# A transformer layer pipeline on one core: four written-out engine orders and the PSUM banks laid out anew, and the first input turned inside the first attention

## The reference, cut to what matters

```python
for i in range(DEPTH):                                        # 6
    x = attn_layer(shift_tokens(x), Wqkv[i], q_scale[i], k_scale[i], Wo[i]) + x
    x = ffn_layer(shift_tokens(x), ln_g[i], ln_b[i], W1[i], b1[i], W2[i], b2[i]) + x

def attn_layer(x, Wqkv, qs, ksc, Wo):                         # 16 heads of 64
    q, k, v = jnp.split(x @ Wqkv, 3, -1)
    q = l2norm(q) * qs
    k = l2norm(k) * ksc
    q = q * cos * scale + rotate_half(q) * sin * scale
    k = k * cos * inv + rotate_half(k) * sin * inv
    out = local_attention(q, k, v)                            # windows of 32, each sees itself and the one before
    return out @ Wo

def ffn_layer(x, g, bln, W1, b1, W2, b2):
    xn = (x - mu) / jnp.sqrt(var + 1e-05) * g + bln
    a, gate = jnp.split(xn @ W1 + b1, 2, -1)
    return a * gelu(gate) @ W2 + b2
```

## Time and profile before

| what | value |
|---|---|
| median of 3 runs | 1480.26 us (1478.79 to 1480.74) |
| the profiled execution, its own time | 1482.22 us |
| span of its instructions | 1480.4 us |
| PE matmul busy | 1422.5 us, 96%, 25844 instructions (214 of them before 54.4 us) |
| ACT busy | 1371.5 us, 93% |
| DVE busy | 1331.4 us, 90% |
| POOL busy | 1257.3 us, 85% |
| mean granted TensorE clock | 0.990 of full speed |

### The profile page before, as it was taken

How to read it: one execution, slowest core, us unless ns; L and a number is a source line. 1 busy time by engine, 2 the same in 40 slices (tenths; PEclk the granted TensorE clock), 3 DMA queues, 4 the chain that set the end, 5 groups by cost and what they waited for, 6 DMA issues and landing times.

```text
span 1480.4 us, 65611 instructions
## 1 busy us (share of the span) xinstructions
PE 1422.5 (96%) x25844; PEld 1278.0 (86%) x25844; DVE 1331.4 (90%) x2411; ACT 1371.5 (93%) x2797; POOL 1257.3 (85%) x1219
## 2 busy tenths in 40 slices
PE   6789999999999999999999999999999999999996
PEld 5578888988998899888888889888898899898886
DVE  7699899999999999999999999999999999999973
ACT  4488899999999999999999999999999999999995
POOL 5498889889898888989888888989898988888871
PEclk9799999999999999999999999999999999999999
DMA  5111121212122211212121221212122111111111
GB/s 150 38 49 52 49 59 49 59 41 62 43 64 58 65 45 49 65 49 64 52 57 44 57 70 51 60 52 54 43 57 68 45 50 41 48 35 51 51 35 40
DMA packets 96187, 80.30 MB, mean 54 GB/s; under 512 B 66282, under 2 KB 79598, under 8 KB 95854
## 3 DMA queue, kind: packets, MB, share of 16 engines
q1 hardware_dynamic: 94990, 75.34, 18.9%
q10 hardware_dynamic: 864, 0.26, 0.1%
HBM read 17.91 MB, written 1.05 MB: 13 GB/s over the span
## 4 chain that ended last, share of the span: by engine, by line
PE 57%; ACT 20%; issue 13%; DVE 9%; DMA 1%; ACTq 0%; POOL 0%; SPq 0%; DVEq 0%; POOLq 0%
PE bank L1132 45%; PE bank L1248 7%; ACT pz L727 4%; PE bank L1276 3%; DVE parts L951 3%; ACT bank L712 3%; ACT sq L651 2%; ACT es L719 2%; DVE n L961 2%; ACT ot L734 1%; DVE newton L970 1%; ACT qt L675 1%; ACT kt L675 1%; ACT gt L756 1%; ACT v L662 1%
## 5 line engine op out<-in xcount | busy, mean ns | idle before, releaser
L480 POOL TENSOR_TENSOR rot<-parts 128x512 f32<-128x512 f32 x384 | 492.0, 1284 | 79.7 <-DVE parts L951 75.9
L951 DVE TENSOR_TENSOR parts<-bank,rtab 128x1024 f32<-128x1024 f32 x384 | 464.7, 1211 | 0.3 <-issue 0.2
L491 POOL TENSOR_TENSOR rot<-rot,rnorm 128x512 f32<-128x512 f32 x384 | 398.6, 1044 | 54.1 <-DVE rnorm L977 54.1
L651 ACT ACTIVATE sq<-bank 128x512 f32<-128x512 f32 x384 | 233.0, 607 | 39.7 <-DVE n L961 20.0
L1132 PE MATMUL bank<-w_hi,x_hi 128*128 128x512 f32 x576 | 256.8, 446 | 7.7 <-DVE x_lo L943 6.7
L961 DVE TENSOR_REDUCE n<-sq 128x8 f32<-128x512 f32 x384 | 254.2, 675 | 4.2 <-ACT sq L651 4.0
L497 POOL TENSOR_TENSOR es<-es,r 128x512 f32<-128x512 f32 x192 | 200.5, 1044 | 37.5 <-DVE r L1003 31.7
L1132 PE MATMUL bank<-w_lo,x_hi 128*128 128x512 f32 x576 | 229.6, 399 | 0.0
L727 ACT ACTIVATE pz<-bank 64x512 f32<-64x512 f32 x384 | 226.2, 589 | 3.1 <-PE bank L1276 0.8
L1132 PE MATMUL bank<-w_hi,x_lo 128*128 128x512 f32 x576 | 228.9, 397 | 0.0
L1248 PE MATMUL bank<-ident,rot 128*128 128x128 f32 x1536 | 215.7, 274 | 5.1 <-issue 4.0
(11 more groups left out here) (91 smaller groups left out, 2985.7 us busy)
## 6 DMA issues: line engine op xcount, KB each, us to landing
vb<-v SPq DMA_DIRECT2D x96, 384.0 KB, 3.7
w_new<-in_Wqkv SPq DMA_DIRECT2D x36, 256.0 KB, 3.0
vb<-v SPq DMA_DIRECT2D x48, 128.0 KB
w_o<-in_Wo SPq DMA_DIRECT2D x12, 256.0 KB
xin<-x_tok SPq DMA_DIRECT2D x48, 64.0 KB, 2.1
xs<-x_tok SPq DMA_DIRECT2D x48, 64.0 KB, 2.7
xin<-x_tok SPq DMA_DIRECT2D x48, 56.0 KB, 2.1
xs<-x_tok SPq DMA_DIRECT2D x48, 56.0 KB, 2.1
```

The lines of the kernel that those rows point to most:

```text
L480: g.tensor_tensor(rot[:, i * CH:(i + 1) * CH].rearrange(halves, z=2, c=HD), parts[:, b:b + CH].rearrange(halves, z=2, c=HD), parts[:, b + ...
L491: g.tensor_tensor(c, c, over(r, CHH, DH), ALU.mult).then_inc(s_sc[i], 1)
L651: a.activation(sq[:, (i % 2) * CH:(i % 2 + 1) * CH], bank[QK_BANK[i]][:, :], ACT.Square)\
L951: d.tensor_tensor(parts[:, b:b + 2 * CH].rearrange("p (w h c) -> p w h c", w=2, c=DH), heads(bank[QK_BANK[i]][:, :]).unsqueeze(1).to_broad ...
```

## The change

The header has new banks, and `SEEDED` is gone with its ident products. `DEEP`, the number of passes after the last step, goes from 7 to 5, since POOL and SP handle their parts in other passes; `take_x` waits for another value chunk.

```diff
-DEEP = 7
+DEEP = 5
-QK_BANK, T_BANK = (7, 6, 3, 5, 4, 2, 1, 3), (0, 0, 5, 4, 7, 6, 7, 0)
-V_BANK, P_BANK, O_BANK = (2, 5, 1, 0), (7, 1, 7, 1), (5, 6, 4, 4)
-S_BANK, W_BANK, H_BANK = ((2, 3), (3, 2)), (4, 6), (0, 5, 6)
-SEEDED = (2, 3,)
-XIN_BANK, N_BANK, D_BANK = 6, 4, 1
-LAST_N2, LAST_SC = (3, 7), (3, 6)
+QK_BANK, T_BANK = (3, 2, 3, 6, 7, 5, 1, 6), (1, 4, 4, 0, 4, 7, 0, 4)
+V_BANK, P_BANK, O_BANK = (5, 5, 1, 2), (4, 0, 1, 4), (4, 5, 1, 0)
+S_BANK, W_BANK, H_BANK = ((2, 3), (3, 2)), (0, 7), (1, 7, 5)
+XIN_BANK, N_BANK, D_BANK = 6, 7, 6
+LAST_N2, LAST_SC = (3, 7), (3, 7)
...
-                act.wait_ge(s_vp[2], done(n - 2))
+                act.wait_ge(s_vp[3], done(n - 2))
```

```diff
             sp.wait_ge(s_zero, 2)
+            for c in range(2, 4):
+                qkv_weights(0, c)
+            load_x(0, True)
+            for c in range(4, WCH):
+                qkv_weights(0, c)
+            for c in range(2):
+                qkv_weights(1, c)
+            up_weights(1)
...
-            for s in (-1, 0, 1):
-                first_attention(s)
-            for s in range(2, SEQS + 1):
-                first_attention(s)
-            pe.wait_ge(s_a["done"], SEQS)
-            pe.wait_ge(s_zero, 2)
-            pe.wait_ge(s_w, 2 * 16 * WLOADS)
-            for b in SEEDED:
-                mm(bank[b][:, :], ident[:, :], w_o[:, 0:CH])
...
+            for s in range(-1, SEQS):
+                first_attention(s)
+            pe.wait_ge(s_a["v"], SEQS)
+            first_turn_p(SEQS - 1)
+            take_in(0, True)
+            first_values(SEQS - 1)
+            pe.wait_ge(s_a["done"], SEQS)
+            pe.wait_ge(s_zero, 2)
+            pe.wait_ge(s_w, 2 * 16 * WLOADS)
```

As it stands in the diff, PE's part around `values(n-2, 0)`:

```diff
+                if live(n - 2):
+                    freed((s_qte[7], n - 2))
                     turn_p(n - 2, 0)
                     scores(n - 2, 1)
                 if live(n - 3):
                     freed((s_mid[0], n - 3))
                     values(n - 3, 3)
                 if live(n - 2):
-                    freed((s_hm[1], n - 5), (s_rot[1], n - 1, 8, 3), (s_v[1], n - 2))
+                    freed((s_pte[0], n - 2, 4, 0))
                     values(n - 2, 0)
```

More of the change, by code:

```diff
@@ L158, in program @@
         bank = [ctx.enter_context(nc.psum_tensor(f"bank{i}", [P, CH], F32)) for i in range(8)]
-        pQ = bank[0:2]
-        pT, pS, pP, pO, pF = bank[3:8]
+        pF = bank[XIN_BANK]
+        pQ0, pQ1, pT, pS, pP, pO = [bank[i] for i in range(8) if i != XIN_BANK][0:6]
+        pQ = (pQ0, pQ1)
         s_first = sem("s_first")
@@ L348, in shifted, with load_x @@
                 sp.dma_start(dst[:, :, 0:h], src[:, :, 0:h]).then_inc(signal, 16)
-            def load_x(n):
+            def load_x(n, ahead=False):
+                if (n == 0) != ahead:
+                    return
                 if n < SEQS:
@@ L795, in iteration @@
                 if live(n - 2):
-                    freed((s_rot[1], n - 1, 8, 5), (s_sub[0], n - 2, 4, 0))
-                    seed(n - 2, 1, 1)
+                    exps(n - 2, 0)
+                    take_qk(n - 2, 5)
+                    take_qk(n - 2, 4)
+                    copy_v(n - 2, 3)
+                    exps(n - 2, 1)
+                if live(n):
+                    take_x(n)
                 if live(n - 1):
@@ L801, in iteration @@
                     gelu(n - 5, 1)
+                if live(n - 2):
+                    freed((s_sub[1], n - 2, 4, 1))
+                    seed(n - 2, 1, 0)
+                    take_qk(n - 2, 7)
+                    freed((s_v[3], n - 2))
+                    seed(n - 2, 1, 1)
+                if live(n - 5):
+                    gelu(n - 5, 2)
+                if live(n - 1):
+                    next_hi(n - 1)
+                if live(n - 5):
                     gelu(n - 5, 0)
+                    exp_and_log()
                 if live(n - 2):
                     take_p(n - 2, 0)
-                if live(n):
-                    next_hi(n)
-                if live(n - 5):
-                    gelu(n - 5, 2)
-                    exp_and_log()
-                if live(n - 2):
-                    exps(n - 2, 2)
+                if live(n - 1):
+                    square(n - 1, 7)
                 if live(n - 3):
@@ L1072, in iteration @@
                 if live(n - 1):
[L1073 removed]
+                    squares(n - 1, 6)
+                if live(n - 2):
+                    maxima(n - 2, 2)
+                if live(n - 5):
+                    gated(n - 5, 0)
                 if live(n - 2):
                     maxima(n - 2, 3)
[L1076 removed]
+                    less_max(n - 2, 2)
                 if live(n - 1):
[L1078 removed]
                     squares(n - 1, 7)
                 if live(n - 2):
[L1081 removed]
                     less_max(n - 2, 3)
@@ L1191, in first_attention, with take_in @@
                     first_values(s - 1)
-            for s in (-1, 0, 1):
+            def take_in(n, ahead=False):
+                if (n == 0) != ahead:
+                    return
+                pe.wait_ge(s_xin[n % 2], 64 * (n // 2) + 64)
+                x = buffer(xin, n, LEN)
+                for T in range(TILES):
+                    last = t.transpose(bank[XIN_BANK][:, T * P:(T + 1) * P], x[:, T * P:(T + 1) * P], ident[:, :])
+                last.then_inc(s_xt, 1)
+            for s in range(-1, SEQS):
                 first_attention(s)
-            for s in range(2, SEQS + 1):
-                first_attention(s)
+            pe.wait_ge(s_a["v"], SEQS)
+            first_turn_p(SEQS - 1)
+            take_in(0, True)
+            first_values(SEQS - 1)
             pe.wait_ge(s_a["done"], SEQS)
@@ L1212, in align_block @@
                 t.addr_align(BLOCK, offset=slot, max_nops=0)
-            def take_in(n):
-                pe.wait_ge(s_xin[n % 2], 64 * (n // 2) + 64)
-                x = buffer(xin, n, LEN)
-                for T in range(TILES):
-                    last = t.transpose(bank[XIN_BANK][:, T * P:(T + 1) * P], x[:, T * P:(T + 1) * P], ident[:, :])
-                last.then_inc(s_xt, 1)
             def product(n, o, T, c):
```

377 lines of the change are left out of this document (176 added, 201 removed).

## The result

The new kernel takes **1549.57 us** (median of four runs, 1547.10 to 1553.76), the kernel before 1480.50 in the same session. The ratio is 1.0467, 95% interval 1.0448 to 1.0485: slower by 69 us. The prediction had slower by 13, 1493 us in a range of 1469 to 1510. The span of the profiled execution is 1545.5 us against 1480.4.

A forecast was written before the change was run, and what follows sets the result against it. The prediction took a closed loop of waits between PE and ACT through take_p to bound the new step. Head -4.8, middle +15.3 and last layer +2.1 sum to +12.6, giving 1493 us, range 1469 to 1510.

The forecast's parts named there:

- The head: Start of the kernel: four seeds gone, first input turned during the first attention, first product near 50.6; -4.8 us.
- The loop through take_p: Steady step: PE's chunk 2, ACT's stretch to take_p, PE's values(n-2, 0); 28.80 us without split, 29.43 with; +15.3 and +2.1.
- the split: ACT's split of a weight chunk, in seven of eight steps, now ahead of take_p; 0.63 us in ACT's stretch.
- Following each PE group to the ACT group that frees its bank: Method used on the steady step to find the loop that the new orders tighten; one loop stood out.
- On this loop DVE has no part; I count 0 for it: Steady step: DVE's long waits for gelu shrink, but this was priced at 0.
- So PE's own work stays: Steady step: PE's four turns of mode are as many as before, so its work is unchanged at 28.45 us.
- (c): Rival, steady step: same stretch with further waits, on less_max or DVE; half a microsecond more a step, 1513 us; chance 0.12.
- The bound of the loop: Error given for the steady step's loop from reading its starts: +-0.35 us a step, +-14 us over 41 steps.

The follow-up runs named there:

- a44_xg: New kernel with the alignment slot at 44 instead of 28 and xg_lo ahead of rotate(n, 2) on DVE; 1504.81 us, ratio 1.0159.
- a_slot60: New kernel with only the alignment slot changed, 60 instead of 28; 1528.40 us, ratio 1.0323.
- a_slot44: New kernel with only the alignment slot changed, 44 instead of 28; 1524.98 us, a single run.
- b_slot0: Kernel before with only the alignment slot changed, 0 instead of 24; 1501.71 us, ratio 1.0136.
- b_head: Kernel before with only the head's part: first input loaded and turned earlier, four seeds gone; 1477.22 us, ratio 0.9975.
- a44_xg_split: New kernel with slot 44, xg_lo ahead of rotate(n, 2), and ACT's weight-chunk split moved behind take_o(n-3, 3); 1492.26 us, ratio 1.0072.

## Why the prediction was wrong

**The head** was right: -4.8 forecast, -4.6 measured on its own, with the first product 5.8 us earlier in the one trace and 4.3 in the other.

**The loop through take_p** was right in its terms (but for the split, 0.52 us and not 0.63) and wrong in its place. Its 29.43 and 28.80 us stand in a44_xg as 29.40 and 28.88. The new kernel's mean of 30.34 hides it; it shows there only in the few steps without a hole. "Following each PE group to the ACT group that frees its bank" is the step that failed: banks are freed by DVE too. The diff has N_BANK = 7 and QK_BANK[4] = 7, and PE's order waits for s_xg ahead of project(n-1, 4); in DVE's new order xg_lo stands behind two rotates, 2.34 us in the row above. "On this loop DVE has no part; I count 0 for it" was true of that loop and answered the wrong question. Loop X has DVE for nearly half its length: moving xg_lo ahead of one of the two rotates gave 29.4 us back (a_xg). In the last layer it also takes in the 1.10 us add to acc, and steps there reached 31.0 us, where I had expected the shortest ones.

**"So PE's own work stays"** is the second step that failed. It counted instructions, and these are the same. It did not ask when they arrive. align_block stood in the diff with 24 changed to 28 and moved from the start of PE's pass to its end, and I priced neither. The hole is worth 21 to 25 us in the new order (a_slot60, a_slot44) and can be brought into the old one (+20, b_slot0).

**How the 69 us add up.** They don't as a sum, because the limits lie over one another: -24.6 for the slot alone, -29.4 for xg_lo alone, -44.8 for both (1549.57 to 1504.81), -57.3 with the split moved (1492.26). What is then left over b_head, which has the same head, is 15 us. In the two traces it is 16.0, and by stages: 5.0 in the first three steps (84.3 us against 79.3; holes over 0.4 us in the fill take 5.7 against 2.4), 4.4 in the middle (29.07 against 28.94 a step), 7.6 in the next nine, and 0.9 less outside them. Why the first four of the last nine steps stay at 29.3 us in a44_xg_split and at 29.6 in a44_xg, where the prediction had 28.80, is not settled; holes and waits for xg_lo of 0.3 us are both there. The new banks, and the new orders of POOL and SP, were not tried by themselves, so what they add to these 15 us is not known.

**The rivals.** (c), a longer loop with further waits, had the right kind. It named DVE and less_max, but as half a microsecond more on the same loop. The bound of the loop, +-0.35 us a step, held only for the loop I had found. It was no bound for loops I had not found, and the range went by it.

## What to carry to other kernels

When an order written by hand changes its banks, follow every release of every bank, from whichever engine, and close each into a loop. A loop found with the right length is no proof that it is the longest one. Where a kernel aligns its instructions, the slot is a number to be measured anew with each order: it was worth 20 to 57 us here and costs nothing to change. And before an instruction moves forward on an engine that is over 90% busy, say what it makes late.

## What the hardware showed unexpectedly

PE's instruction blocks can be late in steady state. The Trainium skill (Runtime: NRT & Kernel Launch, Instruction fetch mechanics) says that PE's instructions come in 16 KiB blocks of 256, fetched by its sequencer while it works, and calls the cost of crossing an edge mostly hidden. The packets (16.4 KB) and the hole's shift by 8 matmuls for 16 slots agree with the block; "mostly hidden" does not: 0.73 to 2.36 us in 42 of 48 passes of the new kernel. The kernel before has three such holes, of 0.8 to 2.6 us, but none in its steady steps. All but one of the holes quoted lie in scores or values, where PE uses up its instructions fastest: 256 of them in the 1.4 us of one scores group. Such a hole shows in the profile as idle time of PE behind "issue" inside a group of one kind, with one packet on the instruction queue beside it, whose end is 1.2 to 1.8 us ahead of PE's going on. What makes the sequencer ask for a block is open: 16 slots moved one packet by more than three us, in b_slot0 it comes at two different times with the same slot, and no run here tells why.
